# Keep-choice attention, second pass: products by keys one at a time, averages in halves of 256 columns, accumulator copied between two exponentials

## What is computed

```python
scores = einsum('bhqd,bhkd->bhqk', q, k) * inv_sqrt_d        # 16 heads of 8
attn_weights = softmax(where(causal, scores, -inf))
mean_importance = attn_weights.mean(axis=2)
mean_importance = mean_importance.at[:, :, -64:].set(1.0)
_, idx = top_k(mean_importance, 391)
K_keep, V_keep = k[idx], v[idx]
s2 = einsum('bhqd,bhkd->bhqk', q, K_keep) * inv_sqrt_d
out = einsum('bhqk,bhkd->bhqd', softmax(s2), V_keep)
return out @ w_proj.T
```

## Time and profile before

| | us |
|---|---|
| median of 3 runs | 2573.2 |
| lowest, highest | 2571.56, 2573.89 |
| the profiled execution, its own time | 2577.72 |
| its span in the trace | 2575.9 |
| mean granted TensorE clock (1 is 2.4 GHz) | 0.937 |
| second pass, first score to last copy of the accumulator | 714.9 to 939.9 |

### The profile page before, as it was taken

How to read it: one execution, slowest core, us unless ns; L and a number is a source line. 1 busy time by engine, 2 the same in 40 slices (tenths; PEclk the granted TensorE clock), 3 DMA queues, 4 the chain that set the end, 5 groups by cost and what they waited for, 6 DMA issues and landing times. The chain is left out here.

```text
span 2575.9 us, 30062 instructions
## 1 busy us (share of the span) xinstructions
PE 2190.9 (85%) x9736; PEld 887.6 (34%) x9776; DVE 1707.1 (66%) x2466; ACT 1224.6 (48%) x2450; POOL 705.7 (27%) x666
## 2 busy tenths in 40 slices
PE   8999999977479989887977779978879988878877
PEld 2333334422122224354433234433324436533323
DVE  5666675578877735643482754579994446569995
ACT  4656663168457743221353234356645422246653
POOL 1111111132211110121101010059981013049882
PEclk9999999979789979997988889999999999989999
DMA  4000000011000011000000000022210000012220
GB/s 164 1 1 1 1 1 1 13 38 42 9 2 1 1 53 46 1 1 1 0 1 0 1 0 1 1 92 89 94 57 1 1 1 2 1 63 97 91 81 17
DMA packets 25050, 68.65 MB, mean 27 GB/s; under 512 B 3584, under 2 KB 9792, under 8 KB 24128
## 3 DMA queue, kind: packets, MB, share of 16 engines
q1 hardware_dynamic: 24272, 66.23, 7.6%
q10 hardware_dynamic: 624, 0.49, 0.1%
HBM read 58.78 MB, written 1.57 MB: 23 GB/s over the span
## 5 line engine op out<-in xcount | busy, mean ns | idle before, releaser
L3884 POOL TENSOR_TENSOR l_drive<-l_du,l_bsb 128x1024 f32<-128x1024 f32 x126 | 296.3, 2374 | 39.8 <-DVE l_du L3785 26.3
L3636 DVE TENSOR_TENSOR_SCAN l_state<-l_decay,l_drive 128x1024 f32<-128x1024 f32 x128 | 289.9, 2277 | 10.0 <-ACT l_decay L3577 9.3
L3466 PE MATMUL l_py<-l_state,w_const 128*128 128x512 f32 x512 | 254.5, 623 | 41.7 <-DVE l_state L3644 29.9
L244 POOL TENSOR_TENSOR l_nx_small<-l_nx_small,w_norm 128x4 f32<-128x4 f32 x50 | 53.3, 1067 | 844.0 <-DVE l_nx_small L237 844.0
L406 ACT ACTIVATE l_probs<-l_psp,l_stats 128x512 f32<-128x512 f32 x256 | 173.1, 683 | 147.1 <-DVE l_stats L416 147.1
L3577 ACT ACTIVATE l_decay<-l_delta,l_a 128x511 f32<-128x511 f32 x256 | 164.9, 680 | 121.9 <-DVE l_state L3636 121.7
L1409 DVE TENSOR_REDUCE l_tops<-l_ring 128x2 f32<-128x1024 f32 x128 | 151.5, 1220 | 45.6 <-PE l_ring L1400 45.2
L414 DVE TENSOR_REDUCE l_stats<-l_psp 128x2 f32<-128x1024 f32 x128 | 156.1, 1220 | 29.3 <-PE l_psp L366 28.9
L867 DVE SCALAR_TENSOR_TENSOR l_product<-l_psu,w_gated,l_first 128x512 f32<-128x512 f32 x104 | 78.0, 750 | 131.7 <-ACT l_first L841 131.3
L1481 ACT ACTIVATE l_shared<-l_ring 128x512 f32<-128x512 f32 x256 | 138.9, 598 | 47.1 <-PE l_ring L1471 46.9
L3466 PEld LDWEIGHTS l_py<-l_state,w_const 128*128 128x128 f32 x512 | 99.9, 199 | 152.6 <-issue 85.2
(11 more groups left out here) (652 smaller groups left out, 4255.7 us busy)
## 6 DMA issues: line engine op xcount, KB each, us to landing
l_bsb<-l_rows SPq DMA_DIRECT2D x64, 512.0 KB, 3.7
l_csb<-l_rows SPq DMA_DIRECT2D x32, 256.0 KB, 3.3
w_gated<-in_gated SPq DMA_DIRECT2D x1, 3297.5 KB, 10.7
w_mha<-in_mha SPq DMA_DIRECT2D x1, 2568.5 KB, 11.4
w_ssm<-in_ssm SPq DMA_DIRECT2D x2, 1171.0 KB, 14.1
l_stack<-l_v SPq DMA_DIRECT2D x48, 48.0 KB
w_moe<-in_moe SPq DMA_DIRECT2D x1, 2248.0 KB, 18.5
l_stack<-keep_parts SPq DMA_DIRECT2D x24, 48.0 KB
```

Source lines behind the costliest of these rows:

```text
L3466: mm = pe.matmul(py[:, t, :], eye, state[:, k % STATES, t, :], start=False, stop=k % NS == NS - 1, skip_group_check=True)
L3636: dve.tensor_tensor_scan(state[:, k % STATES, :, :].rearrange("p t s -> p (t s)"), decay[:, k % 2, :, :].rearrange("p t s -> p (t s)"), dr ...
L3884: pool.tensor_tensor(drive[:, k % RING, :, :], du[:, :, :], bsb[:, k // 2 % RING, k % 2, :].unsqueeze(1).to_broadcast([P, CT, S]), ALU.mult)\
```

## The change

Each slot's two products by keys become two calls, and other work stands between them. TensorE's order in one x was score pair, two products, averages (every second slot), auxiliary work. It is now: first product; score pair; second product; half of the averages. In a slot with shifting or turning (x%4 == 2, x%8 == 0; `turned`) it is: first product; shifting or turning; second product; score pair; half of the averages. The rest (`project_v` and so on) still stands at the end of the slot.

The averages of a round are made in two calls, columns 0 to 255 in the even slot y = 2p+2, columns 256 to 511 in the odd one. The first round of a set (kt = 0, start=True) is still made whole, in the odd slot. A round still ends at the same y as before. On ScalarE the copy of `acc` moves from behind the slot's second exponential to between the two.

```diff
--- before.py
+++ after.py
@@ -1459,41 +1459,53 @@
             kt, u = divmod(r, 2)
             return c, kt, u
 
-        def score_by_keys(pe, x):
+        def score_by_keys(pe, x, i):
             c, kt, u = keys_of(x)
             b, j = divmod(c, KJ)
             T = 2 * j + u
-            if kt == 0 and u == 0:
+            if kt == 0 and u == 0 and i == 0:
                 pe.wait_ge(L["q2"].sem, L["q2"].at(0, 2 * c + 2))
-            for i in range(2):
-                if x:
-                    pe.wait_ge(L["exp2"].sem, L["exp2"].at(0, 2 * x - 1 + i))
-                pe.matmul(ring[:, 4 + i, :], stacks[b][half(i), 1, T, kt * P:(kt + 1) * P],
-                          q2[half(i), (2 * c + u) % 4, :], start=True, stop=True, skip_group_check=True)\
-                    .then_inc(L["st"].sem, 1)
-
-        def exps2(act, x):
+            if x:
+                pe.wait_ge(L["exp2"].sem, L["exp2"].at(0, 2 * x - 1 + i))
+            pe.matmul(ring[:, 4 + i, :], stacks[b][half(i), 1, T, kt * P:(kt + 1) * P],
+                      q2[half(i), (2 * c + u) % 4, :], start=True, stop=True, skip_group_check=True)\
+                .then_inc(L["st"].sem, 1)
+
+        def exps2(act, x, i):
             p = x // 2
-            if x % 2 == 0 and p >= 3:
+            if x % 2 == 0 and i == 0 and p >= 3:
                 act.wait_ge(L["av"].sem, L["av"].at(0, p - 2))
-            for i in range(2):
-                act.wait_ge(L["st"].sem, L["st"].at(0, 2 * x + i + 1))
-                act.activation(probs2[:, p % 3, 2 * (x % 2) + i, :], ring[:, 4 + i, :], ACT.Exp, scale=-1.0)\
-                    .then_inc(L["exp2"].sem, 1)
-
-        def contexts(pe, p):
+            act.wait_ge(L["st"].sem, L["st"].at(0, 2 * x + i + 1))
+            act.activation(probs2[:, p % 3, 2 * (x % 2) + i, :], ring[:, 4 + i, :], ACT.Exp, scale=-1.0)\
+                .then_inc(L["exp2"].sem, 1)
+
+        def contexts(pe, p, lo, hi):
+
             c, kt = divmod(p, TT)
             b, j = divmod(c, KJ)
-            pe.wait_ge(L["exp2"].sem, L["exp2"].at(0, 4 * (p + 1)))
-            if kt == 0:
-                if j == 0:
-                    pe.wait_ge(L["v"].sem, L["v"].at(0, b + 1))
-                if c:
-                    pe.wait_ge(L["c_sb"].sem, L["c_sb"].at(0, c))
+            if lo == 0:
+                pe.wait_ge(L["exp2"].sem, L["exp2"].at(0, 4 * (p + 1)))
+                if kt == 0:
+                    if j == 0:
+                        pe.wait_ge(L["v"].sem, L["v"].at(0, b + 1))
+                    if c:
+                        pe.wait_ge(L["c_sb"].sem, L["c_sb"].at(0, c))
             for g in range(KG):
-                mm = pe.matmul(acc[32 * g:32 * g + 32, :], v[:, b % 2, kt, KG * j + g, :], probs2[:, p % 3, g, :],
+                mm = pe.matmul(acc[32 * g:32 * g + 32, lo:hi], v[:, b % 2, kt, KG * j + g, :], probs2[:, p % 3, g, lo:hi],
                                start=kt == 0, stop=kt == TT - 1, skip_group_check=True)
-            mm.then_inc(L["av"].sem, 1)
+            if hi == S:
+                mm.then_inc(L["av"].sem, 1)
+
+        def add_contexts(pe, y):
+
+            p, odd = divmod(y - 2, 2)
+            if not 0 <= p < PAIRS:
+                return
+            if p % TT == 0:
+                if odd:
+                    contexts(pe, p, 0, S)
+            else:
+                contexts(pe, p, odd * S // 2, (odd + 1) * S // 2)
 
         def take_contexts(act, c):
             act.wait_ge(L["av"].sem, L["av"].at(0, TT * (c + 1)))
@@ -1599,16 +1611,20 @@
                 pe.wait_ge(L["choice"].sem, L["choice"].at(0, L["choice"].per))
                 for x in range(END):
                     y = x - LAG
-                    if x < SLOTS:
+                    turned = x % 4 == 2 and 0 <= x // TT - 1 < B * KT or x % 8 == 0 and 0 <= (x - 24) // 8 < B * KJ
+                    if 0 <= y < SLOTS:
+                        score_by_keys(pe, y, 0)
+                    if x < SLOTS and not turned:
                         score2(pe, x)
-                    if 0 <= y < SLOTS:
-                        score_by_keys(pe, y)
-                    if y >= 3 and y % 2 == 1 and (y - 3) // 2 < PAIRS:
-                        contexts(pe, (y - 3) // 2)
                     if x % 4 == 2 and 0 <= x // TT - 1 < B * KT:
                         shift_rows(pe, x // TT - 1)
                     if x % 8 == 0 and 0 <= (x - 24) // 8 < B * KJ:
                         turn_contexts(pe, (x - 24) // 8)
+                    if 0 <= y < SLOTS:
+                        score_by_keys(pe, y, 1)
+                    if x < SLOTS and turned:
+                        score2(pe, x)
+                    add_contexts(pe, y)
                     if x % 32 == 12 and x < SLOTS:
                         project_v(pe, x // 32)
                     if x % 32 == 20 and x >= 52:
@@ -1642,9 +1658,11 @@
                 for x in range(END):
                     y = x - LAG
                     if 0 <= y < SLOTS:
-                        exps2(act, y)
+                        exps2(act, y, 0)
                     if y % 8 == 2 and 0 <= (y - 10) // 8 < B * KJ:
                         take_contexts(act, (y - 10) // 8)
+                    if 0 <= y < SLOTS:
+                        exps2(act, y, 1)
                     if x % 4 == 3 and 0 <= x // TT - 1 < B * KT:
                         take_q2(act, x // TT - 1)
                     if x % 32 == 13 and x < SLOTS:
```

## The result

The changed kernel takes 2609.0 us (median of 4, 2604.2 to 2609.1), the kernel before 2573.6 in the same comparison (2571.6 to 2575.2): ratio 1.0135, 95% interval 1.0121 to 1.0150. It is slower, as forecast, and 3 us off the predicted 2606. The profiled execution took 2609.1 us, its span is 2607.4, 31.4 more than the span before; the rest of the 35.5 between the medians is that the profiled execution of before lay 4 us above its own median.

A forecast was written before the change was run, and what follows sets the result against it. A ring of waits between TensorE's products and ScalarE's exponentials bounds the kernel. Fourteen groups of 14.33, less 1.6, plus 14.5 for extras give 213.5 against 180.5 us: +33.0, so 2606 us, range 2588 to 2619.

The forecast's parts named there:

- Three rounds for two: TensorE, each slot: first product, score pair, second product take three rounds of 0.22 us, 5.28 us per group of eight slots.
- well off 1.33: Sign against the prediction: slots without auxiliary work taking a time far from the expected 1.33 us.
- rival of two rounds: Different row halves on TensorE overlap out of order, so two rounds suffice: 9 us less, 2597 us; chance 0.10.
- all of those are neighbours in the queue: Argument against out-of-order overlap: every pair of row halves seen running together on TensorE stands side by side in program order.
- the sum: One group of eight slots: TensorE's own work 12.36 us plus bare waits 1.97, together 14.33.
- Averages in halves: TensorE: a split round of averages costs 1.34 us against 1.10 whole; a half can't be under 0.50.
- Auxiliary work without cover: TensorE, between a slot's two products: shifts and turning become bare, 1.28 and 0.68 us per group.
- wait (c): Slot 3's second product waits 0.34 us for the exponential that the accumulator's copy pushes back on ScalarE.
- The extras: project_v, turn_outs and project_out, once in four groups each, become bare with the shift's waits after them: 14.5 us in all.
- The tail, taken at 0: Last twelve slots without score pairs and emptying of the pipeline: between -3 and +5 us, taken as 0.
- The waits stay hidden: Rival: the bare waits of groups and extras vanish, 33 us go, time 2573, no change; chance 0.05.
- Pays off: Rival: ScalarE's idle 0.99 us per pair goes, groups take 10.4 us, 35 us less, 2538 us; chance 0.05.

The follow-up runs named there:

- e4: Changed kernel with the second matmul of every score pair also taken from rows 0-63, so other scores for the second head; 2615.4 us in one execution.
- e5: Changed kernel, TensorE's order untouched, with division, addition to x and copies of q2, v and outs moved earlier; 2574.7 us, ratio 1.0001 to the kernel before.
- e3: Kernel before, its TensorE order kept, with averages halved in three rounds of four and copies, division and addition first in their slot; 2569.6 us, ratio 0.9975.
- e8: Kernel before with copies, division and addition first in their slot, and averages halved only in the round of slots 4 and 5; 2563.0 us, ratio 0.9954.

## Why the prediction came true, step by step

**Three rounds for two: failed, and named as open.** This is the step of the prediction that was wrong, and by its own list of signs ("well off 1.33") it counts against the mechanism, though the total came out. Slots without auxiliary work take 1.11, not 1.33 (831.63 to 832.74). The rival of two rounds had chance 0.10 and its mechanism is what happened; e4 shows it from the other side, at 1.33 with three matmuls on one row half. The Trainium skill ("TensorE: Matmul & The Clock Gate", Part 3, What overlaps and what doesn't) says that matmuls start strictly in program order; both traces have a matmul that starts ahead of, or together with, earlier ones held up on the other rows, so here the measurement decides against that sentence. I had read "all of those are neighbours in the queue" as speaking against it; it was only that no row could show it.

**Why this moved the time so little.** That rival took 9 us off. Of a group, the sum had 14.33 and the trace has 14.16, so 2.4 us off in 14 groups. The saved 0.22 was lost again in most slots, because an engine that TensorE's order doesn't hurry set the end:
- Slot 5: the shift starts 4.54 after slot 4's first product (829.62 to 834.16), exactly as worked out, by VectorE's division. TensorE came 0.22 sooner and waited 1.11 (1.03 of it as idle in the row) instead of 0.89. I had missed this in the rival, where I counted slot 5 among those that save.
- Slot 7: from first to next first product 2.06; the sum has 2.07. TensorE waits 0.95 for q2 (0.88 as idle in the row), not 0.74, which by its own terms should read 0.76.
- Slots 2 and 3: 3.42 (840.36 was slot 2's first product, 843.78 the next slot 4's); the sum has 3.40. The wait (c) is 0.38 in this group and 0.25 in others, against 0.34.
- Slots 0 and 1: 2.51 against 2.66. Here 0.15 was saved, of 0.44: slot 1's second product waits for an exponential.

**Averages in halves: right.** 0.64 long, next work 0.57 later, 0.31 from product to averages. Its lower bound of 0.50 wasn't met.

**Auxiliary work without cover: right.** Turning starts 0.32 behind the product and the second product 0.58 after it; slot 4 takes 2.01, as summed.

**The extras: right in kind, summed 2.7 us too dear.** The groups with project_v, turn_outs and project_out (843.78 to 859.27, 798.70 to 813.69, 813.69 to 829.62) take 1.33, 0.83 and 1.77 more than 14.16, 3.93 together where I had 4.84. The shift's waits behind them are longer than I had: 0.72 for 0.56 and 1.20 for 0.98 from start to start, 0.65 and 1.12 as idle in the rows. Wait (c) is shorter in these groups (0.25 for 0.38), which takes that back. What made them cheaper is slots 0 and 1: with an extra they take its length and 1.11 for each slot, while the same two slots take 2.51 in the group without one, so each extra is 0.29 cheaper than its length. The two waits with their idle time:

```profile
795.77 0.38 PE L1444 MATMUL l_aux<-l_stack,l_eye 128*128 128x512 bf16 x1 [0.65 <-ACT l_v L1552]
...
826.70 0.38 PE L1444 MATMUL l_aux<-l_stack,l_eye 128*128 128x512 bf16 x1 [1.12 <-DVE x L1577]
```

**Sum of the 14 groups.** Predicted 213.5, measured 208.3: 2.4 from the groups, 2.7 from the extras.

**The tail, taken at 0: +3.9, and the head, not counted: +1.8.** The head's part lies behind its first product by keys: `project_v` stands bare there too, and the shift behind it idles 0.67 for the copy of v. (Two earlier shifts idle 0.56 and 0.55 for GpSimd, against the prediction's word that its casts end long before; up to the first product by keys nothing was lost by it.)

From y=116 to the next product that waits for q2 it is 6.8 us before (916.52 to 923.29) and 7.7 after (950.76 to 958.50). That product idles longer for q2 (0.67 before, 1.09 after), but the time is not lost there: from slot 7's first product to it they take 2.05 and 2.06. It is lost in slots 4 to 6, 4.72 before and 5.68 after. Both products in TensorE's timeline of before:

```profile
921.24 0.39 PE L1471 MATMUL l_ring<-l_q,l_stack 64*128 64x512 bf16 x2
...
923.29 0.39 PE L1471 MATMUL l_ring<-l_q,l_stack 64*128 64x512 bf16 x2 [0.67 <-ACT l_q L1454]
```

and after:

```profile
956.44 0.39 PE L1470 MATMUL l_ring<-l_q,l_stack 64*128 64x512 bf16 x2
...
958.50 0.39 PE L1470 MATMUL l_ring<-l_q,l_stack 64*128 64x512 bf16 x2 [1.09 <-ACT l_q L1454]
```

The rest of the tail took 16.0 before and 18.9 after. The window of before:

```profile
923.29:939.28 15.99, 14.16 (x72) 3.58 (x72) 3.86 (x8) 9.98 (x19) 1.02 (x1) 0.79 0.00 0
```

and after:

```profile
958.50:977.43 18.93, 16.65 (x104) 4.70 (x104) 3.86 (x8) 10.19 (x19) 1.02 (x1) 0.73 0.00 1
```

The granted clock is 0.79 in the one and 0.73 in the other. How much of the 2.9 us is clock and how much the order wasn't tried apart. It was named as a possibility within -3 and +5; a value of 0 was too kind, and by luck it stood against the overcharged groups.

So the total was right within 3 us because two errors of about 5 us opposed each other: the groups -5.2, tail and head +5.7, which makes 33.5 of the predicted 33.0. The 3 us that are left are within the scatter of the medians (2604 to 2609 for the changed kernel).

**The rivals.** "The waits stay hidden" gave 2573 for a kernel without (a) to (c) and the extras' waits. e5 is nearly that kernel and took 2574.7: (c) is left in it, and it has two rounds and not three, so the agreement is partly chance. Taking the other waits away needed VectorE's and ScalarE's orders changed, as argued. "Pays off" (10.4 per group) was reached by nothing: the shortest group in any run is 12.14 (e3, without an extra), and e8 needs 12.24 for eight slots.

## What to carry to other kernels

Before work is moved out of a stall, ask what of the other engines' work was sized to fit that stall: here the division, two copies and an addition had been covered by whole averages and a pair of products, and each came bare by 0.4 to 1.1 us. A saving of TensorE time in front of a wait that another engine ends is worth nothing until that engine's step moves forward too; the same halved round brought 0.36 us for eight slots with the copies early and cost 0.23 with them late. Move the copies first, measure, and then shorten the round that holds the turning. And look at the rare groups apart from the common one: e3 and e5 are ahead of the kernel before in a group without an extra and give it back in those with one.

## What the runs showed of the hardware

Matmuls on rows 0-63 and rows 64-127 do not only run side by side when they are neighbours in the program. In the changed kernel the four matmuls of a slot start as two pairs, at 831.63 and 831.86, each a product with one of the score matmuls; in e4 the second product starts together with the first at 804.88 with two score matmuls queued between them, and those start 0.23 later. On the same rows the next matmul started 0.21 to 0.23 later in both.

Entering and leaving the float32 work in four column groups cost the same in all rows shown: 0.31 from product to averages instead of 0.22, and 1.00 or 0.57 from averages of 512 or 256 columns to the next work. Two halves cost 0.14 more than a whole by the latter alone.
